# Reordering the issue of work in a layer-norm, attention and int8 feed-forward kernel on eight cores

## The reference

```
x = L0_attn_x                                  # (8, 2048, 1024) float32
n = layernorm(x)                               # (x - mean) / sqrt(var + 1e-5), no gain
K = n @ Wk;  Q = n @ Wq;  V = n @ Wv           # each 1024 x 1024
scores = Q K^T / 32, causal mask
x = x + softmax(scores) @ V

n = layernorm(x)
x_scale = max(|n|, 1e-6 per row) / 127
x_q = clip(round(n / x_scale), -128, 127)      # int8
out = (x_q @ weight_q^T) * x_scale * weight_scale + bias
x = x + out
```

## Time and profile before

| what | value |
|---|---|
| time, median of 3 runs | 713.8 us (712.16 to 714.63) |
| time of the profiled execution | 713.83 us |
| its span, slowest core (core 5) | 712.3 us |
| spans of the 8 cores | 705.2 to 712.3 us |
| PE, PEld busy | 413.7 us (58%), 192.0 us (27%) |
| DVE, ACT, POOL busy | 250.3 us (35%), 172.6 us (24%), 81.2 us (11%) |
| first part, by the timeline | 0 to 305 us |
| second part, by the timeline | 305 to 712 us |

### The profile page before, as it was taken

How to read it: one execution, slowest core, us unless ns; L and a number is a source line. 1 busy time by engine, 2 the same in 40 slices (tenths; PEclk the granted TensorE clock), 3 DMA queues, 4 the chain that set the end, 5 groups by cost and what they waited for, 6 DMA issues and landing times.

```text
span 712.3 us, 5934 instructions; the slowest of 8 cores (705.2 to 712.3 us)
## 1 busy us (share of the span) xinstructions
PE 413.7 (58%) x2008; PEld 192.0 (27%) x2008; DVE 250.3 (35%) x425; ACT 172.6 (24%) x304; POOL 81.2 (11%) x44
## 2 busy tenths in 40 slices
PE   0015991599179849924356444754674754948345
PEld 0002441244124324411122222322332322414112
DVE  1212443244333423344434244324423424233331
ACT  3221004100410120023222333133223143231420
POOL 2000000000000000011222112211211211202012
PEclk9999996699669969965778788878977988879787
DMA  8992001100110000040111011100110100101001
GB/s 158 193 232 101 1 0 59 60 1 0 61 57 1 0 31 0 1 147 1 59 59 60 0 59 61 59 27 34 60 59 0 60 32 28 60 0 59 1 29 59
DMA packets 11453, 35.07 MB, mean 49 GB/s; under 512 B 896, under 2 KB 896, under 8 KB 11424
## 3 DMA queue, kind: packets, MB, share of 16 engines
q1 hardware_dynamic: 6912, 25.17, 10.2%
q0 software_dynamic: 4512, 9.54, 7.1%
HBM read 31.56 MB, written 8.39 MB: 56 GB/s over the span
## 4 chain that ended last, share of the span: by engine, by line
PE 52%; DVE 13%; ACT 13%; issue 11%; DMA 9%; DVEq 1%; ACTq 0%; POOLq 0%; SPq 0%
PE psF L189 25%; PE psF L484 12%; DMA xbuf<-x 9%; PE psF L560 9%; PE psF L357 6%; ACT xn L447 3%; DVE st L451 3%; ACT xqT L473 2%; DVE st L384 2%; ACT xnbuf L225 2%; DVE x L581 2%; DVE st L363 1%; ACT AT_sb L543 1%; DVE st L388 1%; DVE psF L380 1%
## 5 line engine op out<-in xcount | busy, mean ns | idle before, releaser
L484 PE MATMUL psF<-wqt_sb,xqT 128*128 128x512 bf16 x256 | 85.2, 506 | 142.7 <-ACT xqT L473 142.7
L484 PEld LDWEIGHTS psF<-wqt_sb,xqT 128*128 128x128 bf16 x256 | 30.4, 123 | 192.5 <-issue 182.1
L189 PE MATMUL psF<-xnT,wq_sb 128*128 128x512 bf16 x256 | 66.5, 428 | 24.3 <-DVE xnT L273 24.3
L560 PE MATMUL psF<-Vt,AT_sb 128*128 128x512 bf16 x272 | 62.1, 382 | 21.4 <-ACT AT_sb L543 10.9
L499 POOL TENSOR_TENSOR outf<-t,x1b 128x1024 f32<-128x1024 f32 x16 | 37.5, 2345 | 254.8 <-DVE st L571 145.0
L233 PE MATMUL psBF<-ident_sb,xnbuf 128*128 128x128 bf16 x128 | 13.8, 273 | 89.8 <-ACT xnbuf L225 83.3
L262 ACT ACTIVATE xnbuf<-xbuf 128x1024 bf16<-128x1024 f32 x16 | 16.9, 1056 | 196.8 <-PE psBF L233 133.3
L357 PE MATMUL psF<-KT,QT 128*128 128x512 bf16 (+3 forms) x320 | 63.3, 355 | 0.9 <-DVE Vt L204 0.9
L189 PE MATMUL psF<-wv_sb,xnT 128*128 128x512 bf16 x256 | 55.9, 379 | 0.0
L189 PE MATMUL psF<-xnT,wk_sb 128*128 128x512 bf16 x256 | 55.9, 379 | 0.0
L494 DVE SCALAR_TENSOR_TENSOR t<-psF,st,wsb_sb 128x1024 f32<-128x1024 f32 x16 | 20.5, 1284 | 94.0 <-PE psF L484 69.3
(11 more groups left out here) (60 smaller groups left out, 396.9 us busy)
## 6 DMA issues: line engine op xcount, KB each, us to landing
xbuf<-x SPq DMA_DIRECT2D x16, 512.0 KB, 3.6
xr<-x SPq DMA_DIRECT2D x16, 512.0 KB, 3.9
y<-outf SPq DMA_DIRECT2D x16, 512.0 KB, 2.9
wq_sb<-wq POOLq DMA_DIRECT2D x1, 2048.0 KB, 21.0
wk_sb<-wk POOLq DMA_DIRECT2D x1, 2048.0 KB, 35.0
wv_sb<-wv POOLq DMA_DIRECT2D x1, 2048.0 KB, 47.6
wqt_sb<-wqt POOLq DMA_DIRECT2D x1, 2048.0 KB, 53.9
wsb_sb<-wsb POOLq DMA_DIRECT2D x1, 512.0 KB, 6.2
```

The source lines that it names most:

```text
L189: (lambda t: t.matmul(psQ(b), lhsT, rhs, start=st, stop=sp)))()
L484: (lambda te: te.matmul(psMM[:, sl * 512:(sl + 1) * 512], xqT[jpar][:, kc * 128:(kc + 1) * 128], wqt[:, kc * D + sl * 512: kc * D + (sl + ...
L560: fn = (lambda jj=jj, sl=sl, st=st, sp=sp: (lambda te: te.matmul(psMM[:, sl * 512:(sl + 1) * 512], AT_sb[:, jj * 128:(jj + 1) * 128], Vt[: ...
```

## The change

Both kernels execute the same arithmetic on the same tiles; instruction counts per engine are the same. What differs:

- A buffer `junk` takes the squares of both parts. L262 no longer waits for transposes (only for the last write of `junk`); the writer of `xnbuf` (L225) now waits for them instead. L425 no longer writes to `A_sb`.
- In the first part `flush_evacs` stands behind the statistics of tile t.
- In the second part the order of the code for a round is: scores of i; square, sum and variance of h; mask and maximum of i; 1/std of h; transposes, copy to `xqT[j]`; exponentials of i; feed-forward of j; sum and reciprocal of i; `t2`, add and store of j; `xn1` and largest absolute value of h; transposes and copies of the probabilities; `xqf` and rounding of h; product with V, `x1[i]`, `x1b[i]`.

```diff
+    junk = at("junk_sb", [128, D], BF16)
...
                     scale=stt[:, 5:6], bias=stt[:, 6:7])))(),
-                    inc="ss", waits=[("ss", m_b2)])
+                    inc="ss", waits=[("ss", m_b2), ("ts", m_trT.get(h - 2, 0))])
...
-            if 0 <= h < NT and h % 4 == 0 and h >= 4:
-                flush_evacs(10 ** 9)
             if t < NT:
...
                 m_sq = sch.op("scalar", (lambda par=par, stt=stt: (lambda s: s.activation(
-                    xnbuf[par][:], xbuf[par][:], AF.Square,
+                    junk[:], xbuf[par][:], AF.Square,
                     accum_out=stt[:, 2:3])))(),
-                    inc="ss", waits=[(f"dx{par}", m_dx[t]),
-                                     ("ts", m_trT.get(t - 2, 0))])
+                    inc="ss", waits=[(f"dx{par}", m_dx[t]), ("ss", m_junkw[0])])
+                m_junkw[0] = m_sq
...
+            if 0 <= h < NT and h % 4 == 0 and h >= 4:
+                flush_evacs(10 ** 9)
...
+            if 0 <= h < NT:
+                m_sq2[h] = sch.op("scalar", (lambda hpar=hpar, hst=hst: (lambda s: s.activation(
+                    junk[:], x1[hpar][:], AF.Square,
+                    accum_out=hst[:, 6:7])))(),
+                    inc="ss", waits=[("vs", m_x1[h]), ("ss", m_junkw[0])])
...
+                m_evXQ[j] = sch.op("scalar", (lambda jpar=jpar: (lambda s: s.copy(
+                    xqT[jpar][:], psXQ[:])))(),
+                    inc="ss", waits=[("ts", m_trX[j])])
...
-            if j >= 0:
-                m_evXQ[j] = sch.op("scalar", (lambda jpar=jpar: (lambda s: s.copy(
-                    xqT[jpar][:], psXQ[:])))(),
-                    inc="ss", waits=[("ts", m_trX[j])])
...
+            if 0 <= h < NT:
+                m_xqf[h] = sch.op("scalar", (lambda hpar=hpar, hst=hst: (lambda s: s.activation(
+                    xqf[hpar][:], xn1[:], AF.Identity, scale=hst[:, 14:15])))(),
+                    inc="ss", waits=[("vs", m_inv[h]), ("vs", m_rnd.get(h - 2, 0))])
+                m_rnd[h] = sch.op("vector", (lambda hpar=hpar: (lambda v: v.tensor_scalar(
+                    xq[hpar][:], xqf[hpar][:], C_RND, C_RND,
+                    ALU.add, ALU.subtract)))(),
+                    inc="vs", waits=[("ss", m_xqf[h]), ("ts", m_trX.get(h - 2, 0))])
+
+            if i < NT:
                 w = [("ss", m_evATb[i]), ("ss", m_evATa[i]),
                      ("vs", m_stt2.get(i - 2, 0))]
```

More of the change, by code:

```diff
@@ L157, in build_nc @@
         m_dx = {}
+        m_junkw = [0]
         m_red = {}
@@ L398, in build_nc @@
                 m_b3m[i] = sch.cnt["vs"]
[L399 to L411, removed]
-            if j >= 0:
[L414 to L422, removed]
-            if 0 <= h < NT:
-                m_sq2[h] = sch.op("scalar", (lambda hpar=hpar, hst=hst: (lambda s: s.activation(
-                    A_sb[:, 0:1024], x1[hpar][:], AF.Square,
-                    accum_out=hst[:, 6:7])))(),
-                    inc="ss", waits=[("vs", m_x1[h])])
-                sch.op("vector", (lambda hst=hst: (lambda v: v.scalar_tensor_tensor(
-                    hst[:, 8:9], hst[:, 6:7], 1.0 / D, hst[:, 7:8],
-                    ALU.mult, ALU.subtract)))(),
-                    inc="vs", waits=[("ss", m_sq2[h]), ("vs", m_mm2h[h])])
-                m_rv2[h] = sch.cnt["vs"]
+            if 0 <= h < NT:
                 sch.op("scalar", (lambda hst=hst: (lambda s: s.activation(
@@ L446, in build_nc @@
                 m_b22[h] = sch.cnt["ss"]
+            if j >= 0:
+                w = [("vs", m_rnd[j]),
+                     ("ss", m_evATb.get(i - 1, m_evXQ.get(j - 1, 0)))]
+                for c in range(KC):
+                    fn = (lambda c=c, jpar=jpar: (lambda te: te.transpose(
+                        psXQ[:, c * 128:(c + 1) * 128],
+                        xq[jpar][:, c * 128:(c + 1) * 128], ident[:])))()
+                    m_trX[j] = sch.op("tensor", fn,
+                                      inc=("ts" if c == KC - 1 else None),
+                                      waits=(w if c == 0 else ()))
+                m_evXQ[j] = sch.op("scalar", (lambda jpar=jpar: (lambda s: s.copy(
+                    xqT[jpar][:], psXQ[:])))(),
+                    inc="ss", waits=[("ts", m_trX[j])])
@@ new lines, in build_nc @@
+            if j >= 0:
+                w = [("ss", m_evXQ[j]), ("dwt", m_wqt),
+                     ("vs", m_x1.get(j + 1, 0)), ("vs", m_stt2.get(j - 1, 0))]
+                first = True
+                for kc in range(KC):
+                    for sl in range(2):
+                        st = (kc == 0)
+                        sp = (kc == KC - 1)
+                        fn = (lambda kc=kc, sl=sl, st=st, sp=sp, jpar=jpar:
+                              (lambda te: te.matmul(
+                                  psMM[:, sl * 512:(sl + 1) * 512],
+                                  xqT[jpar][:, kc * 128:(kc + 1) * 128],
+                                  wqt[:, kc * D + sl * 512: kc * D + (sl + 1) * 512],
+                                  start=st, stop=sp)))()
+                        m_ffn[j] = sch.op("tensor", fn,
+                                          inc=("ts" if (sp and sl == 1) else None),
+                                          waits=(w if first else ()))
+                        first = False
@@ L463, in build_nc @@
                 m_inv[h] = sch.cnt["vs"]
-                m_xqf[h] = sch.op("scalar", (lambda hpar=hpar, hst=hst: (lambda s: s.activation(
-                    xqf[hpar][:], xn1[:], AF.Identity, scale=hst[:, 14:15])))(),
-                    inc="ss", waits=[("vs", m_inv[h]), ("vs", m_rnd.get(h - 2, 0))])
-                m_rnd[h] = sch.op("vector", (lambda hpar=hpar: (lambda v: v.tensor_scalar(
-                    xq[hpar][:], xqf[hpar][:], C_RND, C_RND,
-                    ALU.add, ALU.subtract)))(),
-                    inc="vs", waits=[("ss", m_xqf[h]), ("ts", m_trX.get(h - 2, 0))])
```

129 lines of the change are left out of this document (61 added, 68 removed).

## The result

| | before | changed |
|---|---|---|
| time, median of the runs | 713.82 us (8 runs, 712.16 to 714.63) | 590.36 us (8 runs, 589.65 to 591.36) |
| ratio, 95% interval | | 0.8274 [0.8263, 0.8284] |
| span of the slowest core | 712.3 us (core 5) | 589.0 us (core 2) |
| spans of the cores | 705.2 to 712.3 | 581.2 to 589.0 |

The kernel takes 17% less time; 589 us had been forecast. Some executions of a kernel are about 5% longer, with one half of the chip at a lower clock, and every time and comparison here leaves these out. First the page of the changed kernel: its busy times, its chain by line, and the group of the feed-forward matmuls (out<-in, count | busy, mean ns | idle before and what ended it).

The account below looks back on a forecast made before the run. It took latency of an engine-changing chain as the bound, with PE waiting for ACT's copy to `xqT`. Span 712.3 - 24.1 - 32.9 - 72.4 + 3.5 = 586.4; with 1.5 around it 588, plus 1 for the clock 589 us; range 575 to 606.

Parts of the forecast that it names:

- Where the copy to `xqT` can start: Second part: copy no longer queues on ACT; feed-forward starts 6.4 us earlier in round 8, 8.3 in round 15.
- Late rounds: Rounds 8 to 15: PE and its copies set them; product with V starts earlier, 72.4 us less in all.
- The product's length in rounds 13 to 15: Product with V: 1 us added because the clock may fall in the 3 to 4 us stretch ahead of it.
- Early rounds: Rounds 1 to 7: `x1` waits for DVE's chain through the rounding, 17.1 us a round; 32.9 us less.
- Tail: After `x1[15]`: last tile's statistics now stand behind `t2[14]` on DVE; 3.5 us longer.
- First part: Gaps between projection blocks shrink by 8.8, 8.1 and 7.2 us; 24.1 us less.
- (a): Rival: clock falls ahead of every feed-forward, each staying at some 5.4 us; 599 us total, chance 0.16.
- (b): Rival: clock stays high in rounds 2 to 7 too, 1.9 us for six rounds; 577 us total, chance 0.10.
- (c): Rival: reordering only moves waits; exponentials, `xn1` and DVE's chain set every late round; 604 us total, chance 0.11.
- (d): Rival: granted clock goes to its low level in the projection blocks, slower than before; up to 766 us, chance 0.01.
- (e): Rival: peak-current limit of 13/16 clock lengthens the four projection blocks by 41 us; 630 us total, chance 0.03.
- (f): Rival: second part gains nothing, something other than order held `xqT`; 690 us total, chance 0.02.

Follow-up runs that it names:

- filled: Changed kernel plus 6 matmuls of no use between the transposes of the probabilities and the product with V in rounds 13 to 15: 584.64 us, ratio 0.8181.
- the first part alone: Only the first-part edits (squares into `junk`, `flush_evacs` behind the statistics) on the kernel before: 690.41 us, ratio 0.9681.
- the second part alone: Only the second-part reorder, with `junk`, on the kernel before: 612.46 us, ratio 0.8579.

## Why the prediction was right, point by point

- **Where the copy to `xqT` can start.** Predicted 3.98 after `x1` in round 8 and 5.95 in round 15; the feed-forward at 5.2 and 7.2. Measured for the feed-forward 5.08 and 539.17 - 531.91 = 7.26. Right, and putting the copy back cost 71 us.
- **Late rounds.** The product with V was forecast to start 10.7, 10.9, 11.4, 12.3, 13.1, 14.1 and 14.8 us after `x1` in rounds 9 to 15 (the starts before less the gains named); measured 10.6, 10.8, 11.3, 12.1, 12.9, 13.9 and 14.7. Every one within 0.3. Round 8 was off by 1.6 (12.2 instead of 10.6), because the clock fell: the step that took the clock as still high with 3.0 us between scores and feed-forward was wrong for round 8. It had been rested on the earliest fall seen within one idle stretch (2.65 us). The stretch came out at 2.64 us, and the clock was indeed high to its end; the fall came 1.2 us into the feed-forward. It is no sharp limit: on core 7 of the same execution, with the same stretch, the clock stayed (last section), and on the other seven it fell.
- **The product's length in rounds 13 to 15.** I allowed 1 us for a clock fall; on the slowest core it was 4.7 (1.7, 1.5, 1.5). The mechanism was named, as a rule against the change: the Trainium skill ("TensorE: Matmul & The Clock Gate", Part 4: PE-mode transpose) says that transposes do not count as activity as matmuls do. The trace is in line with it, 7.89 us unfilled with 14 transposes in the stretch and 6.20 filled; but the fill also cut the idle time ahead of the product from 1.90 to 0.60 us, so no run here tells the transposes from the idle time around them. I should have priced it by the 2 us a round that the prediction named, and not by 1 us in all.
- **Early rounds.** Forecast 17.1 us each, set by DVE's chain; measured 17.8, 17.4, 17.3, 16.9, 17.0 and 17.1 in rounds 2 to 7. (The terms written out there add up to 17.2.) The rows show `x1` following the rounding with no wait, and moving the statistics ahead shortened these rounds. Round 1 took 12.0 instead of 11.1 on this core.
- **Tail.** Forecast +3.5, measured +4.7: the last feed-forward ran almost wholly at the low clock (6.30 us instead of 5.5).
- **First part.** Gaps between blocks forecast at 18.2, 15.7 and 8.2 us; measured 15.4, 16.8 and 8.5 on the profiled core, and 15.4, 15.8 and 8.1 by the median of the eight. The first was wrong because I carried over the slow load of core 5. The sum, 24.1, agrees with 23.7 in the run of the first part alone.
- **Rivals.** (a), the clock falls ahead of every feed-forward, held in rounds 2 to 8 and the tail and not in 9 to 15. (b) did not come. (c) is true of the early rounds only, as the main case had it. (d) and (e), a lower clock in the dense blocks, did not come: the granted clock is 1.00, 0.95, 0.94 and 0.95 in the four blocks of the changed kernel's profiled core, and what is missing to 1.00 stands in the first 4 to 5 us of a block, behind the gap. (f) fell with the copy put back and with the second part alone.
- **Why the total was so close.** Errors cancelled: +4.6 in the first part (2.8 of it in the first gap, where the forecast had the load), -1.3 early, -3.6 late, -1.2 in the tail. The time of a kernel with one slowest core of eight carries such luck: 8 us between cores in one execution.

Of what was to be seen, the mean of the feed-forward's matmuls was wrong: 473 ns, not "nearer 380". Nine of the sixteen groups still met the low clock. Two more signs were missed by a little: the last `t2` came 25.6 us after `x1[15]`, not 23 to 25, and rounds 14 and 15 took 23.4 and 24.6 us, not 23 at most.

## What to carry to other kernels

Where the chain of waits changes engines at every step, list for each engine what stands ahead of the one instruction that PE waits for, and ask which of it PE needs: moving a ready 1 us copy past a chain that waits for another engine gave 71 of 123 us here. A reorder moves the wait too: look at what now stands between the moved instruction and the next result (`x1` behind the rounding, the tail's statistics behind `t2`), and treat the last rounds, where other work no longer covers, by themselves. Then price the clock: after idle time ahead of a burst, part of the burst itself ran at half speed, so a stretch of 2.2 us mostly cost 1.7 us more, and cheap matmuls in the stretch took it back. Last, when a DVE instruction moves, look at what POOL does at its new place: beside an add there the rounding took 2.5 us instead of 0.69.
